# q and k turned by VectorE in blocks of 32x32 instead of by TensorE, in a fused attention and FFN layer

## The chip, the cores and the metric

One core of one Trainium2 chip. The time is the device time of one execution in microseconds (us). Profiles are of one execution each.

## What is computed

x is [2, 1024, 1024] f32. It is normalised along its last axis (xn), and the output is x + attention(xn) + FFN(xn):

```python
qkv = clip(einsum('bsd,ed->bse', xn, Wqkv), -8, 8); q, k, v = split(qkv)
q = layer_norm(q) * q_ln_w + q_ln_b          # over all 1024 columns; k alike
q, k, v -> [B, S, 32 heads, 32]
scores = einsum('bqhd,bkhd->bhqk', q, k) * 32**-0.5 + slope[h] * (key - query), causal
out = einsum('bhqk,bkhd->bqhd', softmax(scores), v)
attention = einsum('bsd,ed->bse', out, Wout)
FFN = einsum('bsi,oi->bso', xn, mean|W| * sign(W)) + bias
```

## The kernel before

All engines have programs written out by hand, ordered by semaphores. There are 16 token tiles of 128. To keep f32 accuracy, operands are split into a high and a low f16 half, and a product is made of three passes (high-high, high-low, low-high). `product` (line 1029) makes one tile's product: 8 k-tiles x 3 passes x 2 halves of 512 columns, 48 matmuls.

Stages, in order: FFN product (with the input's turn, line 1018); q, then k, then v; attention; output product. The weights of the next stage are split during the present one by ScalarE (`split_hi`, line 648) and VectorE (`split_lo`, line 803); SP loads them (line 382).

**q and k stage**, per token tile: TensorE makes the product of tile t into one of two pairs of PSUM banks, then turns tile t-1's normalised values with 8 f32 transposes of 128x128 (`turn_qk`, line 1076). VectorE clips the product into SBUF (`clipped`, line 890), takes statistics (line 810, then 815), splits a weight piece (803), and normalises in two passes, `xc - mean` times weight (line 911) and times rstd plus bias (line 914). GpSimd makes rstd between (lines 542 and 568). Of the turned tile in PSUM ScalarE makes the high f16 half (`turn_out`, line 698) and stores it from its own DMA queue (700); VectorE makes the low half (`turned_low`, line 900), which SP stores (`store_low`, line 421). The turned layout in DRAM is `[head, 64 rows, token]`, the 64 rows being 32 dimensions, each high and low: pieces of 128 tokens, 256 bytes.

**Stacks.** Attention works on 16 groups (batch, 4 heads). For each, a stack `ks` (rows: k high, k high or low, k low, 3 rows of the position term) and `qs` (q high and low, q high again, ones, and one row of negated maxima) is loaded from DRAM by `load_part` (line 357), 8 DMAs a group in runs of 1024 tokens for k and 512 for q. Three stacks exist. At the start of the V stage SP issues, in order, the last low half of k, waits for it, six fills of constant rows (483, 484), waits, 24 loads for three stacks, and then the first store of v (`store_v`, line 440), for which the third tile's clip in the V stage waits. In attention ScalarE issues group n+2's loads, one part after each chunk of group n from chunk 3 on.

**Attention**, per group n: 12 chunks of keys against query halves. TensorE makes transposed scores (`scores`, line 1160, and a mask matmul, 1163), ScalarE exponentiates (740), TensorE multiplies by v (1183, 1188, 1193), with GpSimd adding some chunks (599). Between, TensorE makes the natural scores of group n+1 (`maxima`, line 1099), and VectorE reduces them to row maxima (931, 935). The maxima of a query half, 16 rows of 128, are turned (1107, 948) and written by SP as one row of the `qs` stack, `row_a_in` (445) and `row_b_in` (449); group n+1 can't start without its row a, and its fifth chunk (chunk 4) needs row b. SP also carries the softmax sums: `sums_out` (455), a reciprocal on VectorE (978), a store to DRAM (460) and a broadcast load (463). VectorE's program has the reciprocals at fixed places among the maxima. GpSimd normalises (578) and makes the low half of the attention output (588). The order in SP's program is:

```python
            for n in range(GROUPS):
                row_b_in(n)
                if n > 0:
                    sums_out(blk_no(n - 1, 1))
                    recips_in(blk_no(n - 1, 1))
                if n < GROUPS - 1:
                    row_a_in(n + 1)
                sums_out(blk_no(n, 0))
                recips_in(blk_no(n, 0))
```

Of the kernel before, what the change touches and what calls it, by code (L numbers as in the profile page):

```python
# [10 lines left out]
P = 128  # L11
# [11 lines left out]
GH = 4  # L23
# [43 lines left out]
def build_program(nc, x, wqkv_t, wout_t, wffn_t, ffn_bias, q_w, q_b, k_w, k_b,  # L67
                  ident_h, ident_b, mask_nat, mask_tr, q_fill, k_fill, k_extra, out):
    q_scr = nc.dram_tensor("q_scr", [HEADS, 2 * DH, TOK], F16, kind="Internal").ap()
    k_scr = nc.dram_tensor("k_scr", [HEADS, 2 * DH, TOK], F16, kind="Internal").ap()  # L70
# [6 lines left out]
    with ctx:  # L77
# [34 lines left out]
        xl = [f16(split_at + s * DM + DM // 2, DM) for s in range(2)]  # L112
        at += 2 * DM
# [18 lines left out]
        qs = [f16(a, GH * SEQ).rearrange("p (a j t) -> p a j t", a=2, j=GH) for a in stack_at]  # L132
        ks = [f16(a + GH * SEQ // 2, GH * SEQ).rearrange("p (j t) -> p j t", j=GH) for a in stack_at]
# [24 lines left out]
        idf = f32(at, P); at += P  # L158
# [42 lines left out]
        idf_set = sem("idf_set")  # L201
# [134 lines left out]
        LOADS = 8  # L336

        def load_part(eng, n, part):

            b, h0, s = n // NG, n % NG * GH, n % STACKS  # L340
            toks = slice(b * SEQ, (b + 1) * SEQ)
            hq = q_scr[h0:h0 + GH, :, toks].rearrange("j r t -> r j t")
            hk = k_scr[h0:h0 + GH, :, toks].rearrange("j r t -> r j t")
            if part < 2:
                dst, src = ks[s][part:2 * DH:2], hk[0:2 * DH:2]
            elif part == 2:
                dst, src = ks[s][2 * DH:3 * DH], hk[1:2 * DH:2]
            elif part == 3:
                dst, src = ks[s][3 * DH:3 * DH + 3], k_extra[h0:h0 + GH].rearrange("j r t -> r j t")
            else:  # L350
                a, again = (part - 4) // 2, part % 2
                cols = slice(a * HALF, (a + 1) * HALF)
                if again:
                    dst, src = qs[s][2 * DH:3 * DH, a], hq[0:2 * DH:2, :, cols]
                else:
                    dst, src = qs[s][0:2 * DH, a], hq[:, :, cols]
            eng.dma_start(dst, src).then_inc(stack_ld[s], 16)  # L357

        def stack_loaded(n):
            return 16 * LOADS * (n // STACKS + 1)  # L360

# [10 lines left out]
        def _(sp):  # L372
# [43 lines left out]
            def rows_of(scr, part, t):  # L416
                return scr.rearrange("(m h) (d s) t -> s (h d) m t", h=GH, s=2)[part][:, :, bass.ds(t * P, P)]

            def store_low(blk, t, p):
                sp.wait_ge(lo_done, ready(t + NT * (blk - 1)))  # L420
                sp.dma_start(rows_of({Q: q_scr, K: k_scr}[blk], 1, t),
                             tl[p].rearrange("p (m t) -> p m t", t=P)).then_inc(tl_st[p], 16)
# [3 lines left out]
            for blk in (K, V):  # L426
                load_w(blk, 0, 0, 0)
                if blk == V:
                    store_low(Q, NT - 1, 1)
                with sp.Fori(0, NT // 2 - 1) as j:  # L430
                    load_w(blk, j * 2 + 1, 1, j)
                    store_low(blk - 1, j * 2, 0)
                    load_w(blk, j * 2 + 2, 0, j + 1)
                    store_low(blk - 1, j * 2 + 1, 1)
                load_w(blk, NT - 1, 1, NT // 2 - 1)
                store_low(blk - 1, NT - 2, 0)
# [6 lines left out]
            def row_a_in(n):  # L443
                sp.wait_ge(nat_out, use(n, ROWA) + 1 + RB)
                sp.dma_start(qs[n % STACKS][P - 1:P, 0], row_a[n % 2][0:16, :]).then_inc(rowa_ld, 16)

            def row_b_in(n):
                sp.wait_ge(nat_out, (use(n + 1, ROWB) if n < GROUPS - 1 else use(GROUPS, 0)) + 1 + RB)
                sp.dma_start(qs[n % STACKS][P - 1:P, 1], row_b[n % 2][0:16, :]).then_inc(rowb_ld, 16)
# [28 lines left out]
            store_low(K, NT - 1, 1)  # L478
# [3 lines left out]
            for s in range(STACKS):  # L482
                sp.dma_start(qs[s][3 * DH:P].rearrange("p a j t -> p (a j t)"), q_fill).then_inc(fill_ld, 16)
                sp.dma_start(ks[s][3 * DH:P].rearrange("p j t -> p (j t)"), k_fill).then_inc(fill_ld, 16)
# [47 lines left out]
        def _(pool):  # L532
            pool.sem_inc(rstd_done, RING)
# [28 lines left out]

            for blk in (Q, K):
                def qk_step(t, p, j, first=False):
                    g, q = t + NT * blk, t + NT * (blk - 1)
                    variance_plus(g, p, eps_qk)
                    pool.wait_ge(u_done, slot_free(q))
                    nc.gpsimd.tensor_tensor(rs[p], var_eps[p], expo, ALU.pow).then_inc(rstd_done, 1)  # L568

                tile_loop(pool, qk_step)  # L570

# [65 lines left out]
        def _(act):  # L637
# [56 lines left out]
            def turn_out(scr, q, t, p, stores):  # L694

                act.wait_ge(qt_done, ready(q))
                act.wait_ge(th_st[p], stored(stores))
                nc.scalar.activation(th[p], banks(4 + 2 * p, 2), ACT.Copy).then_inc(hi_done, 1)
                act.wait_ge(hi_done, ready(q))
                act.dma_start(scr.rearrange("(m h) (d s) t -> s (h d) m t", h=GH, s=2)[0][:, :, bass.ds(t * P, P)],  # L700
                              th[p].rearrange("p (m t) -> p m t", t=P)).then_inc(th_st[p], 16)

            act.wait_ge(idh_ld, 16)
            nc.scalar.activation(idf, idh, ACT.Copy).then_inc(idf_set, 1)
# [3 lines left out]
            for blk in (Q, K):  # L708
# [3 lines left out]
                def qk_step(t, p, j, first=False):  # L712
                    q = t + NT * (blk - 1)
                    split_hi(blk + 1, t, p, j)
                    if not first:
                        before = (j if p else j - 1) + NT // 2 * (blk - 1)
                        turn_out({Q: q_scr, K: k_scr}[blk], q - 1, t - 1, 1 - p, before)
                    elif blk == K:
                        turn_out(q_scr, NT - 1, NT - 1, 1, NT // 2 - 1)
# [5 lines left out]
            for t in range(NT):  # L725
                p, j = t % 2, t // 2
                split_hi(WO, t, p, j)
                if t == 0:
                    turn_out(k_scr, 2 * NT - 1, NT - 1, 1, NT - 1)
# [59 lines left out]
        def _(dve):  # L789
            for s in (w_lo, stats, xl_done, xtl_out, mm_out, u_done, lo_done):  # L790
# [105 lines left out]
            def turned_low(q, p, stores):  # L896

                dve.wait_ge(hi_done, ready(q))
                dve.wait_ge(tl_st[p], stored(stores))
                nc.vector.tensor_tensor(tl[p], banks(4 + 2 * p, 2), th[p], ALU.subtract).then_inc(lo_done, 1)  # L900

            for blk in (Q, K):
                def qk_step(t, p, j, first=False):
# [12 lines left out]
                    if not first:  # L916
                        turned_low(q - 1, 1 - p, (j if p else j - 1) + NT // 2 * (blk - 1))
                    elif blk == K:
                        turned_low(q - 1, 1, NT // 2 - 1)
# [3 lines left out]
            def maxima(s, pos):  # L923
# [3 lines left out]
                for i, key, width, col in parts:  # L927
                    at = j * 4 + (i if i < 4 else 16 + i - 4 if key == 0 else 32 + i - 4)
# [15 lines left out]
            def row_out(n, at, row, loads):  # L944

                dve.wait_ge(nat_done, at + 1)
                need(dve, loads, 16 * (n - 1))
# [14 lines left out]
            for t in range(NT):  # L962
# [7 lines left out]
                if t == 0:  # L970
                    turned_low(2 * NT - 1, 1, NT - 1)
# [33 lines left out]
        def _(pe):  # L1005
            for s in (xt_done, qt_done):
                pe.sem_inc(s, RING)
# [32 lines left out]
            def block_product(blk, t, p, between=None):  # L1040
                pe.wait_ge(mm_out, slot_free(t + NT * blk))
                product([ps[:, 2 * p + c, :] for c in range(2)],
                        lambda k, a: xnt[:, bass.ds(t, 1), k, a, :].rearrange("p o c -> p (o c)"),
# [36 lines left out]
            pe.wait_ge(idf_set, 1)  # L1080
            for blk in (Q, K):
                pe.wait_ge(w_lo, ready(NT * blk - 1))

                def step(t, p, j, first=False):
                    block_product(blk, t, p)
                    if blk == K or not first:
                        turn_qk(t + (NT * (blk - 1) - 1), 1 - p)
# [3 lines left out]
            def maxima(s, pos):  # L1091
# [38 lines left out]
            for t in range(NT):  # L1130
                if t == 0:
                    block_product(V, t, 0)
                    turn_qk(2 * NT - 1, 1)
                    continue
# [3 lines left out]
                if t == V_FIRST:  # L1138
                    pe.wait_ge(fill_ld, 16 * 2 * STACKS)
                    pe.wait_ge(lo_done, ready(NT * 2 - 1))  # L1140
# [8 lines left out]
            def scores(n, c, j):  # L1149
# [49 lines left out]
            for n in range(GROUPS):  # L1199
                pe.wait_ge(rowa_ld, 16 * (n + 1))  # L1200
                for c in range(NC):
                    if c == QB_END[0] + 1:
                        pe.wait_ge(rowb_ld, 16 * (n + 1))
# [34 lines left out]
def _constants():  # L1238
# [18 lines left out]

    def bf(v):
# [31 lines left out]
```

## Time and profile before

| | us |
|---|---|
| median of three runs (lowest, highest) | 1409.92 (1408.61, 1413.5) |
| the profiled execution, its own time | 1414.06 |
| its span, first to last instruction | 1412.3 |
| TensorE busy | 1341.1 (95%) |
| VectorE busy | 791.2 (56%) |
| ScalarE busy | 512.0 (36%) |
| GpSimd busy | 446.0 (32%) |

The mean granted TensorE clock was 0.993 of full speed. Engines are PE (TensorE; PEld is its weight load), DVE (VectorE), ACT (ScalarE), POOL (GpSimd) and SP (SyncE, which only issues DMAs); a q behind a name, as in SPq, marks what the queue of that engine issues. Busy shares are averages over stages; what a change in a stage is worth is read from that stage.

### The profile page before, as it was taken

The numbers are of one execution on the slowest core, as the hardware profiler recorded it, in microseconds if no ns is written. First come the engines' busy times: TensorE is split into PE (matmuls) and PEld (weight loads), VectorE is DVE, ScalarE is ACT, GpSimd is POOL, SyncE is SP. The second block draws the span as 40 slices with busy tenths as digits, with TensorE's granted clock in tenths as the row PEclk, the third lists the DMA queues.
The fourth block names the chain that finished last, engine by engine and source line by source line (L and its number), as shares of the span: only waits on it lengthen the run. The fifth ranks groups of instructions, "written<-read, shape, count | busy, mean of one in ns | idle before, by whom it ended". The sixth has DMA issues, their size and how long they took to land.

```text
span 1412.3 us, 36370 instructions
## 1 busy us (share of the span) xinstructions
PE 1341.1 (95%) x15012; PEld 678.3 (48%) x15012; DVE 791.2 (56%) x1794; ACT 512.0 (36%) x1019; POOL 446.0 (32%) x313
## 2 busy tenths in 40 slices
PE   5799999999999999699999999989999999999998
PEld 2344444444454444244345555555555555444443
DVE  4677266655566661112578778878877788201111
ACT  5444111111111110000037767767777777700000
POOL 1222000000000000000005555555544445697665
PEclk9999999999999999899999999999999999999999
DMA  5445122223222225712122333332333332144543
GB/s 214 156 158 198 70 53 67 67 72 77 61 74 67 70 71 134 195 68 81 54 62 57 90 87 81 89 79 79 84 89 87 87 87 60 46 170 136 165 148 119
DMA packets 143799, 137.99 MB, mean 98 GB/s; under 512 B 81969, under 2 KB 110769, under 8 KB 143474
## 3 DMA queue, kind: packets, MB, share of 16 engines
q1 hardware_dynamic: 79199, 99.55, 23.3%
q10 hardware_dynamic: 64467, 36.50, 10.1%
q8 instruction: 104, 1.70, 0.5%
q14 instruction: 29, 0.24, 0.1%
HBM read 93.42 MB, written 42.21 MB: 96 GB/s over the span
## 4 chain that ended last, share of the span: by engine, by line
PE 77%; DMA 9%; DVE 6%; issue 3%; ACT 2%; SPq 2%; POOL 0%; DVEq 0%; ACTq 0%; POOLq 0%
PE ps L1029 49%; PE ps L1099 7%; PE ps L1160 6%; DMA arena<-arena 5%; PE ps L1183 5%; PE ps L1188 4%; DVE ps L931 2%; PE ps L1076 2%; PE ps L1163 1%; DMA arena<-q_scr 1%; SPq L357 1%; PE ps L1193 1%; DMA v_scr<-arena 1%; ACT arena L663 1%; PE ps L1018 1%
## 5 line engine op out<-in xcount | busy, mean ns | idle before, releaser
L1029 PE MATMUL ps<-arena 128*128 128x512 f16 x3584 | 792.7, 381 | 17.9 <-DVE arena L890 11.8
L1029 PEld LDWEIGHTS ps<-arena 128*128 128x128 f16 (+1 forms) x3584 | 348.8, 98 | 437.2 <-issue 17.3
L740 ACT ACTIVATE arena<-ps 128x512 f32<-128x512 f32 (+3 forms) x768 | 339.6, 498 | 146.0 <-PE ps L1163 92.9
L599 POOL TENSOR_TENSOR arena<-arena 128x2048 f32<-128x2048 f32 (+1 forms) x48 | 201.8, 4204 | 390.8 <-ACT arena L740 388.4
L931 DVE CUSTOM_DVE_ANT_0 ps<-ps,arena 128x128 f32<-128x128 f32 (+3 forms) x512 | 239.4, 518 | 58.2 <-PE ps L1099 56.0
L1160 PE MATMUL ps<-arena 128*32 128x512 f16 (+3 forms) x3072 | 255.3, 327 | 4.0 <-ACT arena L740 2.5
L1099 PE MATMUL ps<-arena 127*32 127x512 f16 (+3 forms) x3072 | 237.3, 327 | 14.7 <-DVE arena L931 10.2
L648 ACT ACTIVATE arena<-arena 128x512 f32 (+1 forms) x64 | 40.1, 629 | 492.2 <-DMA arena<-in_wqkv_t 317.0
L890 DVE TENSOR_SCALAR arena<-ps 128x1024 f32<-128x1024 f32 x48 | 58.8, 1225 | 216.9 <-PE ps L1029 187.6
L935 DVE TENSOR_REDUCE arena<-ps 128x1 f16<-128x512 f32 x256 | 162.9, 682 | 15.7 <-PE ps L1099 15.7
L1183 PE MATMUL ps<-arena 128*32 128x512 f32 (+3 forms) x1536 | 160.8, 485 | 0.5 <-issue 0.3
L542 POOL TENSOR_TENSOR small<-small 128x1 f32<-128x1 f32 x48 | 10.0, 207 | 463.1 <-DVE small L815 463.1
L1160 PEld LDWEIGHTS ps<-arena 128*32 128x32 f16 x3072 | 95.8, 96 | 77.0 <-issue 29.1
L1163 PE MATMUL ps<-arena 128*32 128x128 bf16 x2048 | 123.2, 218 | 0.0
L1099 PEld LDWEIGHTS ps<-arena 127*32 127x32 f16 x3072 | 86.8, 96 | 68.0 <-DVE arena L931 21.1
L995 DVE SCALAR_TENSOR_TENSOR arena<-ps,arena 128x1024 f32<-128x1024 f32 x16 | 19.6, 1224 | 154.5 <-PE ps L1029 131.8
L1188 PE MATMUL ps<-arena 128*32 128x512 f32 (+3 forms) x1024 | 96.4, 445 | 0.0
L1163 PEld LDWEIGHTS ps<-arena 128*32 128x32 bf16 x2048 | 63.0, 97 | 51.2 <-issue 32.0
L931 DVE DVE_READ_ACCUMULATOR2_ANT arena<- 128x1 f16 x512 | 73.3, 143 | 0.0
L810 DVE BATCH_NORM_STATS2 small<-arena 128x6 f32<-128x512 f32 x96 | 61.6, 683 | 7.0 <-DMA arena<-in_x 5.9
L911 DVE SCALAR_TENSOR_TENSOR arena<-arena,small 128x1024 f32<-128x1024 f32 x32 | 41.1, 1285 | 33.3 <-POOL small L568 33.3
L803 DVE SCALAR_TENSOR_TENSOR arena<-arena 128x512 f32 (+1 forms) x64 | 44.0, 689 | 15.7 <-DVE small L810 11.6
(53 smaller groups left out, 785.9 us busy)
## 6 DMA issues: line engine op xcount, KB each, us to landing
arena<-in_x SPq DMA_DIRECT2D x32, 512.0 KB, 5.3
arena<-in_wqkv_t SPq DMA_DIRECT2D x48, 256.0 KB, 2.9
arena<-k_scr ACTq DMA_DIRECT2D x39, 256.0 KB
base_scr<-arena SPq DMA_DIRECT2D x16, 512.0 KB, 2.9
v_scr<-arena SPq DMA_DIRECT2D x16, 512.0 KB, 2.9
arena<-r_scr SPq DMA_DIRECT2D x32, 256.0 KB
arena<-base_scr SPq DMA_DIRECT2D x16, 512.0 KB, 4.4
out_dram<-arena SPq DMA_DIRECT2D x16, 512.0 KB, 6.2
```

What stands on the lines that cost most here:

```text
L599: nc.gpsimd.tensor_tensor(acc[:, :, at:HALF], former, p32[k % PSLOTS][:, :, 0:w], ALU.add)\
L740: nc.scalar.activation(p32[k % PSLOTS][:, j, 0:w], ps[:, TRB[x % RB], 0:w], ACT.Exp, scale=SCALE).then_inc(exp_done, 1)
L810: ins = nc.vector.bn_stats(bst[p][:, 6 * c:6 * c + 6], xc[p][:, c * HALF:(c + 1) * HALF])
L890: nc.vector.tensor_scalar(dst[p], banks(2 * p, 2), lim, -lim, ALU.min, ALU.max)\
L931: ins = nc.vector.tensor_tensor_reduce(tile, tile, mnat[:, HALF - width:HALF], scale=-1.0, scalar=3e38, op0=ALU.add, op1=ALU.min, accum_ou ...
L935: ins = nc.vector.tensor_reduce(negm[s % 2][:, at:at + 1], tile, AX, ALU.max, negate=True)
L1029: ins = nc.tensor.matmul(dst[c], lhs(k, a), wparts[:, k, b, c * HALF:(c + 1) * HALF], start=(k == 0 and (a, b) == order[0]), stop=(k == KT ...
L1099: ins = nc.tensor.matmul(ps[r:r + DH, NATB[use(s, pos) % RB], col:col + width], q[0:P - 1, i // 4, j, at:at + DH], k[0:P - 1, j, key:key + ...
L1160: ins = nc.tensor.matmul(dst, k[:, j, t * P + r:t * P + r + DH], q[:, qb, j, at:at + w], start=True, stop=not diagonal)
L1163: ins = nc.tensor.matmul(dst[:, 0:P], idb[:, r:r + DH], mtr, start=False, stop=True)
L1183: ins = nc.tensor.matmul(dst(O_BANK, j, at), v[:, t, j, :], p[:, j, 0:w], start=first, stop=last)
L1188: ins = nc.tensor.matmul(dst(S_BANK, j, at), ones_w, p[:, j, 0:w], start=first, stop=last and qb == 0)
```

## The change

VectorE turns q and k instead of TensorE. Its transpose works on blocks of 32x32 within the tile: partition 32a+d, column 32h+x of the result `ut` holds token 32a+x, dimension d of head h. ScalarE then makes the high half from `ut` in SBUF, GpSimd (no longer VectorE) the low half. The scratch in DRAM becomes `[batch, a, tile, high/low, d, 1024]`, so a store writes rows of 2 KB; a stack's columns run (a, tile, head, 32 tokens), and its load reads pieces of 4 heads x 32 tokens, 256 bytes, in 5 DMAs and not 8. In q and k the product takes the tiles of the two batches in turn (`tile=p * QT + j`). TensorE reads tokens in order from the stack by a three-step pattern (tile, a, token in the block). Rows a and b go into the stack as four DMAs each. The position rows are laid out to suit on the host. The core of the diff:

```diff
-    q_scr = nc.dram_tensor("q_scr", [HEADS, 2 * DH, TOK], F16, kind="Internal").ap()
+    q_scr = nc.dram_tensor("q_scr", [BATCH, P // DH, QT, 2, DH, HEADS * DH], F16, kind="Internal").ap()
...
-        qs = [f16(a, GH * SEQ).rearrange("p (a j t) -> p a j t", a=2, j=GH) for a in stack_at]
+        qs = [f16(a, GH * SEQ).rearrange("p (a t j x) -> p a t j x", a=P // DH, j=GH, x=DH) for a in stack_at]
...
-        LOADS = 8
+        LOADS = 5
+        ROW_PARTS = 16 * (P // DH)
...
+            b, g, s = n // NG, n % NG, n % STACKS
+            cols = slice(g * GH * DH, (g + 1) * GH * DH)
+            both = [scr[b, :, :, :, :, cols].rearrange("a t s d x -> (s d) (a t) x") for scr in (q_scr, k_scr)]
+            q, k = [stack[s].rearrange("p a t j x -> p (a t) (j x)") for stack in (qs, ks)]
+            if part == 0:
+                dst, src = k[0:DH], both[1][0:DH]
+            elif part == 1:
+                dst, src = k[DH:3 * DH], both[1]
             elif part == 2:
+                dst, src = ks[s][3 * DH:3 * DH + 3].rearrange("p a t j x -> p (a t j x)"), k_extra[g]
             elif part == 3:
+                dst, src = q[0:2 * DH], both[0]
             else:
+                dst, src = q[2 * DH:3 * DH], both[0][0:DH]
...
             def row_a_in(n):
                 sp.wait_ge(nat_out, use(n, ROWA) + 1 + RB)
-                sp.dma_start(qs[n % STACKS][P - 1:P, 0], row_a[n % 2][0:16, :]).then_inc(rowa_ld, 16)
+                for a in range(P // DH):
+                    sp.dma_start(qs[n % STACKS][P - 1:P, a, 0:QT // 2].rearrange("p t j x -> p (t j) x"),
+                                 row_a[n % 2][0:16, a * DH:(a + 1) * DH]).then_inc(rowa_ld, 16)
...
+            def low_part(q, p, stores):
+
+                pool.wait_ge(hi_done, ready(q))
+                pool.wait_ge(tl_st[p], stored(stores))
+                nc.gpsimd.tensor_tensor(tl[p], ut[p], th[p], ALU.subtract).then_inc(lo_done, 1)
+
             for blk in (Q, K):
                 def qk_step(t, p, j, first=False):
                     g, q = t + NT * blk, t + NT * (blk - 1)
                     variance_plus(g, p, eps_qk)
                     pool.wait_ge(u_done, slot_free(q))
                     nc.gpsimd.tensor_tensor(rs[p], var_eps[p], expo, ALU.pow).then_inc(rstd_done, 1)
+                    if not first:
+                        low_part(q - 1, 1 - p, (j if p else j - 1) + NT // 2 * (blk - 1))
...
-                nc.scalar.activation(th[p], banks(4 + 2 * p, 2), ACT.Copy).then_inc(hi_done, 1)
+                nc.scalar.activation(th[p], ut[p], ACT.Copy).then_inc(hi_done, 1)
...
-            def turned_low(q, p, stores):
-
-                dve.wait_ge(hi_done, ready(q))
-                dve.wait_ge(tl_st[p], stored(stores))
-                nc.vector.tensor_tensor(tl[p], banks(4 + 2 * p, 2), th[p], ALU.subtract).then_inc(lo_done, 1)
...
+                    dve.wait_ge(u_done, ready(q))
+                    dve.wait_ge(lo_done, slot_free(q))
+                    nc.vector.transpose(ut[p], u[p]).then_inc(qt_done, 1)
...
+            def by_tile(dst):
+
+                return dst.rearrange("p (t a x) -> p t a x", a=P // DH, x=DH)
+
+            def tiles_of(stack, j, at, width):
+
+                return stack[:, :, at // P:(at + width) // P, j].rearrange("p a t x -> p t a x")
...
-            def turn_qk(q, p):
-
-                pe.wait_ge(u_done, ready(q))
-                pe.wait_ge(lo_done, slot_free(q))
-                for m in range(KT):
-                    ins = nc.tensor.transpose(ps[:, 4 + 2 * p + m // 4, (m % 4) * P:(m % 4 + 1) * P],
-                                              u[p][:, m * P:(m + 1) * P], idf)
-                ins.then_inc(qt_done, 1)
...
                     for r in range(0, P, DH):
-                        at = i % 4 * P + r
-                        ins = nc.tensor.matmul(ps[r:r + DH, NATB[use(s, pos) % RB], col:col + width],
-                                               q[0:P - 1, i // 4, j, at:at + DH], k[0:P - 1, j, key:key + width],
-                                               start=True, stop=True)
+                        dst = ps[r:r + DH, NATB[use(s, pos) % RB], col:col + width]
+                        ins = nc.tensor.matmul(by_tile(dst), q[0:P - 1, r // DH, i, j],
+                                               tiles_of(k[0:P - 1], j, key, width), start=True, stop=True)
...
-                    ins = nc.tensor.matmul(dst, k[:, j, t * P + r:t * P + r + DH], q[:, qb, j, at:at + w],
+                    ins = nc.tensor.matmul(by_tile(dst), k[:, r // DH, t, j], tiles_of(q, j, q0, w),
```

## Rows read from the trace of the kernel before

**Rows 1.** The page, part 4: the last chain's shares by line.
```profile
PE ps L1029 49%; PE ps L1099 7%; PE ps L1160 6%; DMA arena<-arena 5%; PE ps L1183 5%; PE ps L1188 4%; DVE ps L931 2%; PE ps L1076 2%; PE ps L1163 1%; DMA arena<-q_scr 1%; SPq L357 1%; PE ps L1193 1%; DMA v_scr<-arena 1%; ACT arena L663 1%; 
```

**Rows 2.** The last chain in order of time: start, us, what.
```profile
184.72 10.36 PE ps L1029 x48
...
330.75 10.37 PE ps L1029 x48
...
344.47 10.53 PE ps L1029 x48
...
513.15 10.37 PE ps L1029 x48
...
570.17 11.35 DMA v_scr<-arena
...
582.82 85.85 PE ps L1029 x390
```

**Rows 3.** Waits of PE, 740 to 1150 us: us in total, times, longest.
```profile
PE ps L1099 <- DVE arena L931: 10.2, 9, 1.8
PE ps L1099 <- DMA arena<-q_scr: 3.0, 3, 1.8
```

**Rows 4.** Timeline of a q tile: start, us, engine, line, operation [idle before].
```profile
318.48 1.04 PE L1076 MATMUL ps<-arena 128*128 128x128 f32 x8
318.68 1.23 DVE L890 TENSOR_SCALAR arena<-ps 128x1024 f32<-128x1024 f32 x1 [2.86 <-PE ps L1029]
...
322.73 0.55 POOL L568 TENSOR_TENSOR small<-small 128x1 f32<-128x1 f32 x1 [0.16 <-POOL small L542]
323.40 1.28 DVE L911 SCALAR_TENSOR_TENSOR arena<-arena,small 128x1024 f32<-128x1024 f32 x1 [1.10 <-POOL small L568]
324.72 1.28 DVE L914 SCALAR_TENSOR_TENSOR arena<-arena,small 128x1024 f32<-128x1024 f32 x1
325.92 1.22 DVE L900 TENSOR_TENSOR arena<-ps,arena 128x1024 f16<-128x1024 f32 x1
```

**Rows 5.** Timeline of attention, and line 941's durations (ns, min/median/max).
```profile
786.40 1.16 POOL L588 TENSOR_TENSOR arena<-arena 128x512 f16<-128x512 f32 x1
786.79 0.79 DVE L941 TENSOR_TENSOR arena<-arena 128x16 f16<-128x16 f16 x1
...
L941 DVE TENSOR_TENSOR arena<-arena x16: 166/210/982, 722.6 to 1210.5; 128x16 f16<-128x16 f16 x16
```

**Rows 6.** Timeline between k and v; v's store from the page, landing last.
```profile
535.82 0.63 ACT L648 ACTIVATE arena<-arena 128x512 f16<-128x512 f32 x1 [9.77 <-DMA arena<-in_wout_t]
...
542.31 0.40 SPq L421 DMA_DIRECT2D k_scr<-arena  x1
...
554.55 2.01 SPq L357 DMA_DIRECT2D arena<-k_scr  x3
...
v_scr<-arena SPq DMA_DIRECT2D x16, 512.0 KB, 2.9
```

**Rows 7.** ScalarE's DMA queue: packets, MB, share; 200:335 (256 B stores), 760.5:766 (512 B loads).
```profile
q10 hardware_dynamic: 12985, 3.27, 10.7%
...
q10 hardware_dynamic: 1088, 0.62, 44.0%
```

**Rows 8.** Timeline of one group: SP's issues and VectorE's reciprocal.
```profile
838.43 0.55 SPq L463 DMA_DIRECT2D arena<-r_scr  x1
839.02 0.55 SPq L445 DMA_DIRECT2D arena<-arena  x1
839.66 0.55 SPq L455 DMA_DIRECT2D arena<-arena  x1
...
846.04 0.25 DVE L978 RECIPROCAL arena<-arena 128x16 f32<-128x16 f32 x1 [2.89 <-DMA arena<-arena]
```

**Rows 9.** The same two in the last group, with no stack loads about.
```profile
1217.65 0.55 SPq L455 DMA_DIRECT2D arena<-arena  x1
...
1219.51 0.25 DVE L978 RECIPROCAL arena<-arena 128x16 f32<-128x16 f32 x1 [8.00 <-DMA arena<-arena]
```

More of the change, by code:

```diff
@@ L112, in build_program @@
         xl = [f16(split_at + s * DM + DM // 2, DM) for s in range(2)]
+        ut = [f32(split_at + s * DM, DM) for s in range(2)]
         at += 2 * DM
@@ L131, in build_program @@
         stack_at = [turn_at - 4 * DM, turn_at, ln_at]
-        qs = [f16(a, GH * SEQ).rearrange("p (a j t) -> p a j t", a=2, j=GH) for a in stack_at]
-        ks = [f16(a + GH * SEQ // 2, GH * SEQ).rearrange("p (j t) -> p j t", j=GH) for a in stack_at]
+        qs = [f16(a, GH * SEQ).rearrange("p (a t j x) -> p a t j x", a=P // DH, j=GH, x=DH) for a in stack_at]
+        ks = [f16(a + GH * SEQ // 2, GH * SEQ).rearrange("p (a t j x) -> p a t j x", a=P // DH, j=GH, x=DH)
+              for a in stack_at]
         PSLOTS = 4
@@ L157, in build_program @@
         ones_w = f32(at, DH); at += DH
-        idf = f32(at, P); at += P
         assert at <= WORDS, at
@@ L532, in _ @@
         def _(pool):
-            pool.sem_inc(rstd_done, RING)
+            for s in (rstd_done, lo_done):
+                pool.sem_inc(s, RING)
             for col, value in ((expo, -0.5), (eps_x, LN_EPS), (eps_qk, LN_EPS * (SX * SW) ** 2),
@@ L715, in qk_step @@
                     if not first:
-                        before = (j if p else j - 1) + NT // 2 * (blk - 1)
-                        turn_out({Q: q_scr, K: k_scr}[blk], q - 1, t - 1, 1 - p, before)
+                        turn_out(blk, q - 1, 1 - p, j if p else j - 1)
                     elif blk == K:
-                        turn_out(q_scr, NT - 1, NT - 1, 1, NT // 2 - 1)
+                        turn_out(Q, NT - 1, 1, NT // 2 - 1)
                 tile_loop(act, qk_step)
@@ L789, in _ @@
         def _(dve):
-            for s in (w_lo, stats, xl_done, xtl_out, mm_out, u_done, lo_done):
+            for s in (w_lo, stats, xl_done, xtl_out, mm_out, u_done, qt_done):
                 dve.sem_inc(s, RING)
@@ L927, in maxima @@
                 for i, key, width, col in parts:
-                    at = j * 4 + (i if i < 4 else 16 + i - 4 if key == 0 else 32 + i - 4)
+                    at = i * GH + j + (GH * QT // 2 if key > 0 and i >= QT // 2 else 0)
                     tile = ps[:, NATB[use(s, pos) % RB], col:col + width]
@@ L946, in row_out @@
                 dve.wait_ge(nat_done, at + 1)
-                need(dve, loads, 16 * (n - 1))
+                need(dve, loads, ROW_PARTS * (n - 1))
                 nc.vector.tensor_copy(row[n % 2][0:16, :], bank16(NATB[at % RB])[0:16, 0:P]).then_inc(nat_out, 1)
@@ L1005, in _ @@
         def _(pe):
-            for s in (xt_done, qt_done):
-                pe.sem_inc(s, RING)
+            pe.sem_inc(xt_done, RING)
             pe.wait_ge(idh_ld, 16)
@@ L1084, in step @@
                 def step(t, p, j, first=False):
-                    block_product(blk, t, p)
-                    if blk == K or not first:
-                        turn_qk(t + (NT * (blk - 1) - 1), 1 - p)
+                    block_product(blk, t, p, tile=p * QT + j)
                 tile_loop(pe, step)
@@ L1130, in _ @@
             for t in range(NT):
[L1131 to L1134, printed above, removed]
                 if t < V_FIRST:
@@ L1256, in _constants @@
         rest = rest - k_extra[:, r].astype(np.float64)
+    k_extra = k_extra.reshape(NG, GH, 3, QT, P // DH, DH).transpose(0, 2, 4, 3, 1, 5).reshape(NG, 3, GH * SEQ)
+    k_extra = np.ascontiguousarray(k_extra)
     def bf(v):
```

75 lines of the change are left out of this document (27 added, 48 removed).

## The prediction

> **What bounds the kernel now.** I read the page first. The chain that ended last runs mostly through TensorE, and the products of line 1029 are half of the span; the f32 transposes of line 1076, which the change takes off TensorE, are 2% of it [rows 1]. Then I read the chain in order of time. In the q and k stages it is nothing but products of 10.36 us: the third of q starts at 184.72 and the sixteenth at 330.75, thirteen steps of 11.23 us. So 0.87 us of each step is the turn on TensorE, and nothing else lies between products. K is alike from 344.47 to 513.15. The V stage has one hole: the fifth V product starts at 582.82, behind a store of v that lands 11.35 us after its issue at 570.17 [rows 2]. In attention I read the waits: TensorE is idle for 10.2 us in twelve groups behind VectorE's line 931, and three times, 3.0 us in all, for a stack's last load of q [rows 3].
>
> **The turn leaves TensorE.** There are 32 turns. Fourteen lie between products of q and fifteen between products of k; two, in the last steps of q and k, lie under the wait for VectorE's split of the next weights (the hole ahead of 344.47), and one lies in the V stage ahead of the hole named above. Those three are worth nothing. If TensorE stays the bound, 29 x 0.87 = 25.3 us go.
>
> **VectorE's loop.** I count from the start C of the clip of line 890 (318.68). The rstd of line 568 ends at C+4.60, line 911 starts at C+4.72, and the old subtraction of line 900 starts at C+7.24 and takes 1.22, so VectorE is free at C+8.46 [rows 4]. It loses line 900 and gets a transpose of 128x1024 f32, which waits for line 914 of its own engine (+0.11, as line 914's start behind 911 is 1.32 for a duration of 1.28, where starts without such a wait overlap by 0.08). No row shows the transpose. By the nearest one, a pass over 1024 f32 elements, it takes 1.22; at half that rate, 2.44; how much quicker it could be doesn't matter, since a product of 10.36 is the floor. I take 1.22: C+8.6, under 10.36.
>
> **GpSimd's new subtraction.** It is queued right behind line 568, and what it waits for (ScalarE's high half of the tile before) has long been done, so it starts at about C+4.65, in the same instant as line 911. Its size: line 588 does the same thing, f16 from f32 and f16, on half as many elements in 1.16, so 2.3 us. Nothing of before shows a long GpSimd operation beside line 911, but one pair of rows shows what to expect: line 941 of VectorE reads two operands from SBUF, takes 0.17 at best, took 0.79 when it started inside line 588, and both ended together (787.56 and 787.58) [rows 5]. So a VectorE operation with two SBUF operands stands still until GpSimd is done, its end 0.15 us ahead of what adding would give. Lines 911 and 914 are such operations. If GpSimd goes first, line 911 in effect starts at C+6.80 and not C+4.72; if VectorE goes first, line 914 is held instead, to the same sum. The transpose then starts at 6.80 + 2.52 + 0.11 = C+9.43 and ends at C+10.65, and the next clip starts at C+10.57: I take a step of 10.6, 0.24 above TensorE's. Fifteen steps of each stage pay that: 7.2 us of the 25.3. The term is -18.1 us, between -25.3 (no blocking) and, with a transpose of 2.44 (step 11.8), +18.
>
> The Trainium skill (SBUF — State Buffer, "SBUF: two separate sides") calls this an exclusive lock on a shared port pair, held for the whole instruction, and names VectorE operations with two SBUF inputs; by that rule the trace agrees (0.79 beside 0.17). A reader of the page alone would add the full 2.3 us, where the sum above adds 2.1.
>
> **From K to V.** Let T be the end of the last k product, 523.52. Before, its last low half is issued at 542.31 (T+18.8), because the turn waits for a whole V product; then fills, first load at 554.55 (T+31.0), and the fifth V product at T+59.3 [rows 2, 6]. After: transpose done at T+10.7; ScalarE's high half 1.1 more and, as its queue has a weight piece ahead that comes about then (535.82, T+12.3, and 1.7 sooner now), T+12; GpSimd 2.3; issue at T+14.4, 4.4 sooner. First load at T+26.6. Now the loads: three stacks are 3 x 6144 pieces of 256 B, where they were 3 x 1152 of 1 and 2 KB. Stores in pieces of 256 B took 0.107 x 16 x 135 us / 12985 = 17.8 ns each; loads in pieces of 512 B took 0.44 x 16 x 5.5 / 1088 = 35.6 ns each [rows 7]. These are my two bounds: 20.5 us to 41.0 us for the three stacks on 16 engines. I take 24 ns, nearer the row with the same length, 27.6 us. The store of v is queued behind them (2.9 [rows 6]), and the clip waits for it (1.3, as 1.23 in [rows 4]): fifth V product at T+58.4, against T+59.3. The term is -1 us, between -8 and +12.5. SP's and ScalarE's fewer load instructions (5 for 8) aren't on the path.
>
> The Trainium skill (DMA: Bandwidth & Descriptors, "Specifications") asks for at least 512 B a transfer for line rate. It speaks against this change, which makes the stores long and the larger number of loads short. The 256 B stores here ran at 256 / 17.8 = 14.4 GB/s an engine, exactly the rate of the 512 B loads, so this trace shows no such penalty; no run yet shows it for loads.
>
> **Attention.** Per group SP does in order: reciprocals in (838.43), row a (839.02), sums out (839.66), 0.64 apart; the sums land only at 846.04, where line 978 has held VectorE for 2.89 us, and the maxima of line 931 behind it are what TensorE waits for [rows 3, 8]. Row a is now four DMAs, so the sums are issued 3 x 0.64 = 1.9 us later. But the same DMA takes 1.86 us from issue to line 978 where nothing is ahead of it (1217.65 to 1219.51) [rows 9], so 4.5 us of the 6.4 is queueing behind the reciprocals' broadcast and ScalarE's stack loads. A later issue eats into that queueing, and the loads now stop at chunk 7 instead of 10. Bounds: nothing, and 1.9 x the 14 groups that load stacks = 27 us. I take a quarter, 0.5 a group, +7. Loads that end three chunks sooner take the three waits for q away: -3. Row b's four DMAs come at a group's start and are wanted at its fifth chunk; the products of four chunks hide them, and without that cover it would be up to 1.9 us a group again.
>
> The products of lines 1099 and 1160 read runs of 32 tokens, 64 B, and write PSUM in order. I cost that at nothing, as the rows have no such read; at 10% more on their 13% of the chain [rows 1] it would be 19 us.
>
> **Sum.** -18.1 - 1 + 7 - 3 = -15 us. The profiled execution took 1414.06 (span 1412.3), the median is 1409.92, 0.3% less; the forecast is 1409.92 - 15 = 1395, its own range 1386 to 1405.
>
> **Rivals.**
> - TensorE stays the bound: GpSimd and VectorE don't collide, or the queueing absorbs row a. -25.3 - 3 = -28, 1382; with loads of 17.8 ns 1375. For it: VectorE has 1.9 us of slack before the collision. Against: [rows 5].
> - The row a issues count in full: -18 - 1 + 27 - 3 = +5, 1415, no change to slightly slower. For it: a strictly serial queue. Against: [rows 9].
> - The loads are slow: 35.6 ns, +13.5 on the forecast, 1408.
> - On the other side, the transpose: at 2.44 us VectorE is the bound at 11.8 a step, +18 + 3 = +21, 1431. It decides from 1.7 us on. For it: 32-bit elements through a block reorder, which no row shows; against: all VectorE passes over f32 here run at one rate. The Trainium skill (Vector Engine (DVE) Microarchitecture Reference, "The reshape front-end and per-opcode configuration") says a transpose sustains one element per cycle per lane; no run here shows it yet.
> - The three-step read slows the attention products by 10%: +19, 1414. It decides from about 8%.
>
> **How the numbers follow.** Forecast 0.43, TensorE-bound 0.20, row a in full 0.11, slow loads 0.06, slow transpose 0.10, slow reads 0.10. A difference under 0.3% (4.2 us) can't be told from none. Faster: the first two and the mildest of the slow reads, 0.65; the same: the slow loads, half of the row a case and a little of the slow reads, 0.14; slower, the rest, 0.21. The range, 1376 to 1418, leaves out the slow transpose, the worse half of the slow reads and the very best case.
>
> **What would show it.** Product starts in q and k 10.6 apart, not 10.36 or 11.8; a transpose near 1.2 us; line 911 or 914 at up to 3.4 us instead of 1.28, ending with GpSimd's subtraction; first stack load about 26.6 and the fifth V product about 58 us after the last k product; sums out issued 1.9 us later behind four row a DMAs, with line 978's wait up by about half a microsecond; no TensorE wait for q; mean durations of lines 1099 and 1160 at 0.327 us as before. The prediction falls if the transpose is far from 1.2, if short loads cost more than 36 ns, or if the wait of line 978 grows by the full 1.9.

## The result, and the profile after

The change makes the kernel slower: 1463.65 us, median of four runs (1462.86 to 1467.21), against 1411.71 for the kernel before (four runs). The ratio is 1.0368, with a 95% interval of 1.0328 to 1.0408. The forecast was 1395 us, with a range of 1376 to 1418, so the result lies outside the range and on the other side of the kernel before. The profiled execution took 1462.86 (span 1460.9), 48.6 us more than the span before. The mean granted TensorE clock was 0.975.

From the page of the changed kernel: busy times, its groups for the moved work, and the landing of the weight pieces:

```profile
PE 1322.9 (91%) x14756; PEld 649.4 (44%) x14756; DVE 846.4 (58%) x1794; ACT 510.4 (35%) x1018; POOL 512.4 (35%) x345
...
L916 DVE SCALAR_TENSOR_TENSOR arena<-arena,small 128x1024 f32<-128x1024 f32 x32 | 96.1, 3003 | 33.4 <-POOL small L578 33.4
...
L571 POOL TENSOR_TENSOR arena<-arena 128x1024 f16<-128x1024 f32 x32 | 68.0, 2124 | 9.6 <-ACT arena L713 9.6
...
arena<-in_wqkv_t SPq DMA_DIRECT2D x48, 256.0 KB, 6.2
```

TensorE is less busy than before (1322.9 us against 1341.1), as it should be, and yet the kernel is longer. No engine's busy time explains that: VectorE's rose from 791.2 to 846.4, but it is only 58% of the span. The last row is the surprise: a weight piece of 256 KB takes 6.2 us from issue to landing, where the page of before has 2.9 in the same row. The new transpose, from the groups by line:

```profile
L923 DVE STREAM_TRANSPOSE arena<-arena 128x1024 f32<-128x1024 f32 x32 | 39.9, 1245 | 1.1
```

**Where the time came.** Both traces are cut at the same three events: the end T of the last k product, the start of the fifth V product, the start of the output product. (T is the start of the last k product plus its duration: 512.98 + 10.52 before, 534.57 + 10.53 after.)

| us | T | T to fifth V product | to output product |
|---|---|---|---|
| before | 523.50 | 59.3 | 656.7 |
| forecast, against before | -18.1 | -1 | +4 |
| after | 545.10 | 80.4 | 662.7 |
| measured, against before | +21.6 | +21.1 | +6.0 |

The differences sum to 48.7, the spans differ by 48.6. The q, k and V stages hold the miss; attention is near its forecast.

**One tile of q, after.** The timeline, to set beside [rows 4]:

```profile
322.41 0.63 ACT L663 ACTIVATE arena<-arena 128x512 f32 x1 [11.08 <-DMA arena<-in_wqkv_t]
...
323.40 0.69 DVE L814 SCALAR_TENSOR_TENSOR arena<-arena 128x512 f32 x1 [2.68 <-ACT arena L663]
324.01 0.20 DVE L826 BATCH_NORM_AGGREGATE small<-small 128x2 f32<-128x12 f32 x1
...
324.56 0.55 POOL L578 TENSOR_TENSOR small<-small 128x1 f32<-128x1 f32 x1
325.07 2.13 POOL L571 TENSOR_TENSOR arena<-arena 128x1024 f16<-128x1024 f32 x1
325.23 3.05 DVE L916 SCALAR_TENSOR_TENSOR arena<-arena,small 128x1024 f32<-128x1024 f32 x1 [1.02 <-POOL small L578]
327.37 0.58 SPq L421 DMA_DIRECT2D q_scr<-arena  x1
...
328.64 0.34 SPq L385 DMA_DIRECT2D arena<-in_wqkv_t  x1
...
332.05 4.27 PE L1030 MATMUL ps<-arena 128*128 128x512 f16 x19 [1.95 <-DVE arena L901]
...
335.04 0.63 ACT L663 ACTIVATE arena<-arena 128x512 f32 x1 [11.05 <-DMA arena<-in_wqkv_t]
```

Read it as a circle. ScalarE splits a weight piece (322.41). VectorE, whose program is in order, waits 2.68 us for that to make the low half of the piece (323.40), and only behind it closes the statistics (324.01). GpSimd makes rstd, and behind it the new low half of the tile before (to 327.20). SP stores that (327.37), and behind the store issues the next weight piece (328.64). This lands when ScalarE takes it at 335.04, 6.40 us after its issue. From 322.41 to 335.04 are 12.63 us, and no product is among them. TensorE, which needs 10.5, waits 1.95 for VectorE's clip. With a landing of 2.9, as before, the same circle would take 6.23 + 2.9 = 9.1 us and would be hidden under the product.

The circle is not new. In the kernel before it stands in the same tile, and VectorE, which starts its part at 321.49, finds the high half ready since 320.80:

```profile
320.17 0.63 ACT L648 ACTIVATE arena<-arena 128x512 f32 x1 [9.87 <-DMA arena<-in_wqkv_t]
...
328.17 0.34 SPq L382 DMA_DIRECT2D arena<-in_wqkv_t  x1
...
331.13 0.63 ACT L648 ACTIVATE arena<-arena 128x512 f32 x1 [9.42 <-DMA arena<-in_wqkv_t]
```

One round was 10.96 us there, of which 0.69 were slack, so it needed 10.3 of a step of 11.23. The change made its work shorter (8.00 to 6.23 us up to the issue of the weight piece) and its landing longer (2.96 to 6.40).

The waits from 180 to 560 us (in total, times, longest) say the same, VectorE's first, then TensorE's:

```profile
DVE arena L814 <- ACT arena L663: 69.8, 28, 2.7
```

```profile
PE ps L1030 <- DVE arena L901: 24.1, 15, 2.2
PE ps L1030 <- DVE arena L814: 19.0, 1, 19.0
```

The chain of waits is no help here unless one knows what it hides. Its pieces in order of time alternate between GpSimd's subtraction and a long "issue", in which SP's two issues and the landing of the weight piece have no row of their own:

```profile
312.48 2.13 POOL arena L571
314.61 9.64 issue
...
325.11 2.09 POOL arena L571
327.20 9.67 issue
```

**Why a landing of 6.4.** The DMA share of a stretch (last but one column) is a mean over 16 engines. While the stores of this tile and the weight piece behind them run:

```profile
330.00:331.00 1.00, 0.10 (x1) 0.00 (x0) 1.00 (x2) 0.00 (x0) 0.00 (x0) 1.00 0.64 215
331.00:334.00 3.00, 1.95 (x9) 0.90 (x10) 2.27 (x3) 0.00 (x0) 0.00 (x0) 1.00 0.23 81
```

The first row has a burst over many engines, which is read here as the weight piece (issued at 328.64) on those that are free. After it, 0.23 of 16 is about four engines busy for three microseconds, at 81 GB/s; the piece is there only when they are done. The view that the store writes has the block `a` as its outermost dimension, and that has four values. The Trainium skill (DMA: Bandwidth & Descriptors, "Why a DMA increments its semaphore by 16 and not by 1") says that a DMA is spread over the largest number of engines, up to 16, that divides the outermost dimension (of more than one value) on both sides. By that rule it is four here, and the trace agrees with its 0.23; the experiments below test it.

**From K to V**, timeline after, to set beside [rows 6]:

```profile
574.78 0.63 ACT L663 ACTIVATE arena<-arena 128x512 f16<-128x512 f32 x1 [10.93 <-DMA arena<-in_wout_t]
...
578.59 0.55 SPq L421 DMA_DIRECT2D k_scr<-arena  x1
...
586.11 0.35 SPq L486 DMA_DIRECT2D arena<-in_q_fill  x1
...
595.87 1.11 SPq L355 DMA_DIRECT2D arena<-k_scr  x2
...
618.53 1.63 SPq L439 DMA_DIRECT2D v_scr<-arena  x1
...
624.24 1.23 DVE L901 TENSOR_SCALAR arena<-ps 128x1024 f32<-128x1024 f32 x1 [36.03 <-DMA v_scr<-arena]
```

The store of the last low half is issued at T+33.5 (before T+18.8, forecast T+14.4). The fills wait for it for 7.5 us, which were 2.7 before (542.31 to 545.01). From the first load to the fifth V product at 625.52 are 29.7 us, where 31.8 were forecast: the short loads are not what is slow. The last tile of k is clipped at T+13.1, where before it was at T, because VectorE is by then one tile behind TensorE.

**Attention**, SP and VectorE in one group, to set beside [rows 8]:

```profile
883.31 3.40 SPq L445 DMA_DIRECT2D arena<-arena  x4
886.81 0.59 SPq L458 DMA_DIRECT2D arena<-arena  x1
...
889.66 0.25 DVE L980 RECIPROCAL arena<-arena 128x16 f32<-128x16 f32 x1 [2.32 <-DMA arena<-arena]
```

Row a takes SP 3.40 us of issuing, the sums follow. They now land 2.85 us after their issue, where they took 6.4 in [rows 8]. Over all of attention VectorE waits a little longer for them, 0.43 us a group, where half a microsecond was forecast (722 to 1240 us before, 771 to 1289 after):

```profile
DVE arena L978 <- DMA arena<-arena: 46.8, 15, 9.5
```

```profile
DVE arena L980 <- DMA arena<-arena: 53.3, 15, 9.5
```

### The profile page after: what moved, and what is told of

The parts are those of the page before. It is cut to its first block, busy times and chain, and to the rows that moved or that the text cites. A ratio compares the mean times of both kernels' runs of the same rounds, so it can differ in the third digit from the quotient of the medians.

```text
span 1460.9 us, 35937 instructions
## 1 busy us (share of the span) xinstructions
PE 1322.9 (91%) x14756; PEld 649.4 (44%) x14756; DVE 846.4 (58%) x1794; ACT 510.4 (35%) x1018; POOL 512.4 (35%) x345
## 3 DMA queue, kind: packets, MB, share of 16 engines
q10 hardware_dynamic: 99566, 36.50, 10.6%
## 4 chain that ended last, share of the span: by engine, by line
PE 47%; issue 32%; POOL 7%; DMA 6%; SPq 4%; DVE 4%; ACT 0%; POOLq 0%; ACTq 0%; DVEq 0%
PE ps L1030 20%; PE ps L1096 7%; PE ps L1151 7%; PE ps L1174 6%; PE ps L1179 5%; POOL arena L571 4%; DMA arena<-arena 3%; DVE ps L935 2%; SPq L445 2%; SPq L355 2%; PE ps L1154 1%; PE ps L1184 1%; POOL small L555 1%; POOL small L551 1%; POOL small L546 1%
## 5 line engine op out<-in xcount | busy, mean ns | idle before, releaser
L1096 PE MATMUL ps<-arena 127*32 127x512 f16 (+3 forms) x3072 | 237.6, 328 | 18.3 <-DVE arena L935 16.9
L1151 PEld LDWEIGHTS ps<-arena 128*32 128x32 f16 x3072 | 95.7, 96 | 79.2 <-issue 29.7
L916 DVE SCALAR_TENSOR_TENSOR arena<-arena,small 128x1024 f32<-128x1024 f32 x32 | 96.1, 3003 | 33.4 <-POOL small L578 33.4
L571 POOL TENSOR_TENSOR arena<-arena 128x1024 f16<-128x1024 f32 x32 | 68.0, 2124 | 9.6 <-ACT arena L713 9.6
```

The costliest lines, as they stand in the source:

```text
L571: nc.gpsimd.tensor_tensor(tl[p], ut[p], th[p], ALU.subtract).then_inc(lo_done, 1)
L916: nc.vector.scalar_tensor_tensor(u[p], xc[p], mv[p][:, 0:1], w, ALU.subtract, ALU.mult)\
L1096: ins = nc.tensor.matmul(by_tile(dst), q[0:P - 1, r // DH, i, j], tiles_of(k[0:P - 1], j, key, width), start=True, stop=True)
L1151: ins = nc.tensor.matmul(by_tile(dst), k[:, r // DH, t, j], tiles_of(q, j, q0, w), start=True, stop=not diagonal)
```

## The experiments

Theory 1: the store in rows of 2 KB runs on four DMA engines, the weight piece queued behind it on those engines lands late, and the circle through the queue sets the step. Theory 2: the collision of VectorE and GpSimd, or VectorE's longer loop, sets it. Theory 3: SP's order alone sets it, on however many engines the stores run. For attention, A: the order in which SP issues row a and the sums counts in full; B: the sums wait in the DMA queues anyway, and the order matters little. Ratios are against the kernel before on the same chip; its median was 1411.71, 1409.84 and 1412.99 us in the three sets of runs, so differences of whole times between sets are uncertain by about 3 us.

**a1_store4**: every store of a half as four DMAs of 32 partitions. Each covers one block, so its outermost dimension of more than one value has 32. Bytes, rows of 2 KB and order stay. The low half's store is shown; ScalarE's store of the high half is cut up in the same way.

```diff
-                sp.dma_start(half_of(blk, p, j, 1), tl[p]).then_inc(tl_st[p], 16)
+                for dst, src in halves_of(blk, p, j, 1, tl[p]):
+                    sp.dma_start(dst, src).then_inc(tl_st[p], 16)
```

> The changed kernel with each store of a high or low half of q and k as four DMAs of 32 partitions, and nothing else. Theory 1 (narrow stores): a store whose DRAM side has the four blocks as its outer dimension runs on few of the 16 DMA engines, the weight piece that SP issues behind it lands after 6.2 to 6.4 us and not 2.9, and the loop weight split, rstd, low half, store, weight load closes at 12.6 us a tile. Then the landing goes back to about 3 us, three more issues cost some 1.5 us, the step falls to about 10.7 us, and the time to 1463.6 - 30 x 1.9 = 1407, or 1402 with the last stores ahead of V quicker too. Theory 2 (only the collision of VectorE and GpSimd sets the step): no change, 1460 to 1470. Theory 3 (SP's order alone, whatever the engines): no change or slower by the extra issues.

Measured: 1392.8 us, ratio 0.9886 (0.9862 to 0.9911), 71 us less than the changed kernel. Timeline and DMA share of a tile:

```profile
301.11 3.05 DVE L924 SCALAR_TENSOR_TENSOR arena<-arena,small 128x1024 f32<-128x1024 f32 x1 [1.02 <-POOL small L583]
303.24 1.81 SPq L426 DMA_DIRECT2D q_scr<-arena  x4
...
305.73 0.37 SPq L389 DMA_DIRECT2D arena<-in_wqkv_t  x1
...
308.57 0.63 ACT L670 ACTIVATE arena<-arena 128x512 f32 x1 [8.71 <-DMA arena<-in_wqkv_t]
```

```profile
305.00:306.00 1.00, 1.00 (x7) 0.45 (x5) 0.97 (x2) 0.00 (x0) 0.00 (x0) 1.00 0.52 131
```

Four stores cost SP 1.2 us more of issuing, and the weight piece lands after 2.84 instead of 6.40. The share of 0.52 is over eight engines' worth. The clips are 10.36 apart, TensorE's own pace, and VectorE's line still takes 3.05 beside GpSimd. T is 498.24, 25.3 before that of the kernel before: the whole turn on TensorE is gained. Theory 1 holds; theory 3, which wanted no gain, falls. The time is below the 1402 of theory 1 because the step is 10.36 and not 10.7: neither the collision nor the extra issues cost anything here.

**a5_store2**: the same with two DMAs of 64 partitions (`STORES = 2`); the outermost dimension of each is two.

> The changed kernel with each store of a half as two DMAs of 64 partitions: the suspected cost made larger. Theory 1: if the outer dimension of the DRAM side sets how many engines a DMA uses, each has two instead of four, the two share them, and the store takes twice as long, some 3.3 us more, so the weight piece lands after some 9.6 us and the step grows to about 16: 1463.6 + 30 x 3.3 = 1563. Theories 2 and 3: one more issue of about 0.4 us, at most 1476.

Measured: 1574.99 us, ratio 1.1163 (1.1133 to 1.1192). From the page, and from the windows of a tile:

```profile
arena<-in_wqkv_t SPq DMA_DIRECT2D x48, 256.0 KB, 9.0
```

```profile
322.00:323.00 1.00, 0.00 (x0) 0.00 (x0) 0.96 (x2) 0.00 (x0) 0.00 (x0) 0.74 0.26 94
323.00:324.00 1.00, 0.94 (x3) 0.40 (x4) 1.00 (x2) 0.00 (x0) 0.00 (x0) 0.50 0.13 51
324.00:325.00 1.00, 1.00 (x4) 0.33 (x3) 0.21 (x1) 0.00 (x0) 0.00 (x0) 0.50 0.13 51
```

0.13 of 16 is two engines, and it stands there from 323 to 328: two DMAs a store, and still only two engines, so both ran on the same two. The landing of the weight piece goes 6.2, 9.0, 2.7 us with one, two and four DMAs: it isn't the size or the number of DMAs that counts, but the engines that each one gets. These rows also give a price: 51 GB/s are 25.5 an engine. A tile stores two halves of 256 KB, so four engines are busy with them for 2 x 262,144 / 102 GB/s = 5.1 us, and two for 10.3 (estimates). The step is 16.1 us: SP's stores are issued at 318.30 and 334.39.

**a2_weights_first**: SP issues each weight piece ahead of the low half's store that it stood behind; the stores stay as the change has them.

```diff
                 load_w(blk, 0, 0, 0)
+                load_w(blk, 1, 1, 0)
...
-                    load_w(blk, j * 2 + 1, 1, j)
+                    load_w(blk, j * 2 + 2, 0, j + 1)
                     store_low(blk - 1, j * 2, 0, j)
-                    load_w(blk, j * 2 + 2, 0, j + 1)
+                    load_w(blk, j * 2 + 3, 1, j + 1)
                     store_low(blk - 1, j * 2 + 1, 1, j)
-                load_w(blk, NT - 1, 1, NT // 2 - 1)
```

> The changed kernel with SP issuing each weight piece of the k and v weights as soon as its staging slot is free, one step ahead of the low half's store that stood before it. Theories 1 and 3: the loop through the store is cut, VectorE's own loop with the collision remains, 10.6 us a step, and the time falls by 30 x 2.0 = 60 us to 1404. Theory 2: the collision sets the 12.6 us, so nothing changes, 1464.

Measured: 1401.79 us, ratio 0.9946 (0.9929 to 0.9963). The clips are 10.36 apart here too. Timeline:

```profile
303.42 0.34 SPq L385 DMA_DIRECT2D arena<-in_wqkv_t  x1
...
309.60 0.63 ACT L663 ACTIVATE arena<-arena 128x512 f32 x1 [2.83 <-DMA arena<-in_wqkv_t]
```

The piece still takes 6.2 us, but it is a tile ahead, so nobody behind ScalarE waits for it: the circle is cut at its other joint. What is left of the slow stores shows between K and V: T to the fifth V product is 63.6 us against 55.6 in a1.

**a3_low_vector**: the low half goes back to VectorE, behind the second normalisation; GpSimd makes none, so there is no collision. The stores stay. Of the edit the line itself is shown; it moves from GpSimd's program to VectorE's.

```diff
-                nc.gpsimd.tensor_tensor(tl[p], ut[p], th[p], ALU.subtract).then_inc(lo_done, 1)
+                nc.vector.tensor_tensor(tl[p], ut[p], th[p], ALU.subtract).then_inc(lo_done, 1)
```

> The changed kernel with the low half made by VectorE from SBUF, where the old kernel's subtraction stood (behind line 914, ahead of the transpose), so nothing long runs on GpSimd. Theory 2: the collision is gone, VectorE's loop is 9.8 us, TensorE is the bound at 10.4, time 1463.6 - 30 x 2.2 = 1398. Theories 1 and 3: line 911's 3.05 us becomes 1.28, but the low half is ready later (two passes of 1.28 and one of 1.22 in place of GpSimd's 2.12), the store and the weight load behind it too, and the loop grows from 12.6 to about 14.4: slower, 1463.6 + 30 x 1.8 = 1518.

Measured: 1516.51 us, ratio 1.0768 (1.0738 to 1.0798). Timeline:

```profile
312.40 0.63 ACT L652 ACTIVATE arena<-arena 128x512 f32 x1 [12.89 <-DMA arena<-in_wqkv_t]
...
315.23 1.28 DVE L911 SCALAR_TENSOR_TENSOR arena<-arena,small 128x1024 f32<-128x1024 f32 x1 [1.01 <-POOL small L572]
...
319.14 0.58 SPq L421 DMA_DIRECT2D q_scr<-arena  x1
...
326.65 0.63 ACT L652 ACTIVATE arena<-arena 128x512 f32 x1 [12.67 <-DMA arena<-in_wqkv_t]
```

Line 911 is back at 1.28, and the kernel is 53 us slower than with the collision. The store comes later in VectorE's order, and the circle grows to 14.25 us. Theory 2, which wanted a gain, falls.

**b2_first_low_vector**: a2 and a3 together.

> Weight pieces ahead of the stores as in the run at 1401.8, and the low half on VectorE besides, so that nothing on GpSimd collides with lines 911 and 914. In the run at 1401.8 the step was 10.36 us, TensorE's own, with the collision (3.05 us instead of 1.28) in it, so I expect that taking the collision away gives nothing: 1400 to 1404 (VectorE 9.8 us a step). If the collision still cost what the prediction said, 0.24 us a step, it would be 7 us less, 1395.

Measured: 1401.21 us, ratio 0.9932 (0.9898 to 0.9967), not told apart from a2 alone (0.9929 to 0.9963). With the circle cut, it makes no difference whether GpSimd or VectorE makes the low half: the collision is worth nothing at a step of 10.36.

**a4_sums_first**: the changed kernel, with the sums of the group ahead of the four DMAs of row a in SP's program.

```diff
+                sums_out(blk_no(n, 0))
                 if n < GROUPS - 1:
                     row_a_in(n + 1)
-                sums_out(blk_no(n, 0))
```

> The changed kernel with SP issuing, in each attention group, the sums of the first half ahead of row a's four DMAs. In the changed kernel row a takes 3.4 us of issues ahead of the sums (883.31 to 886.81), which land 2.85 us after their issue. Theory A (serial issues): the sums leave 3.4 us sooner and land as much sooner, VectorE's wait of about 2.7 us a group at the reciprocal goes, and with it most of TensorE's 15 to 17 us behind line 935: 1463.6 - 15 = 1449. Theory B (queueing): they land as late as the broadcast load and the stack loads ahead of them let them, about 7 us after that broadcast's issue as in both traces, and the gain is under 4 us: 1460 or more.

Measured: 1453.54 us, ratio 1.0291 (1.0252 to 1.0329): 10 us less than the changed kernel, nearer A (1449) than B (1460 or more). TensorE's wait behind the maxima from 740 to 1250 us, in the changed kernel and then here:

```profile
PE ps L1096 <- DVE arena L935: 16.9, 14, 1.9
```

```profile
PE ps L1096 <- DVE arena L935: 8.7, 13, 1.4
```

**c1_before_sums_first**: the same edit on the kernel before, where row a is one DMA.

> The kernel before with the sums ahead of row a, which is one DMA there, 0.64 us of issue. Theory A (serial issues): 0.64 us a group sooner, so at most 8 us: 1402. Theory B (queueing): nothing, 1408 to 1411.

Measured: 1409.56 us, ratio 0.9981 (0.9958 to 1.0004), not told apart from none, as B has it. TensorE's wait behind the maxima went from 10.2 [rows 3] to 7.0.

**b5_store4_first_sums**: the three cures together: stores in four, weights first, sums first.

> All three cures in the changed kernel: stores as four DMAs, weight pieces ahead of the stores, sums ahead of row a. q and k are already at TensorE's step with either of the first two, so against 1392.8 (four DMAs alone) only the attention stage changes: 1378 by theory A of the sums (serial issues), 1390 by theory B (queueing).

Measured: 1382.63 us, ratio 0.9785 (0.975 to 0.982). This beats both kernels, the one before by 2.1% and the changed one by 81 us.

All runs, cut at the same events (profiled executions, us):

| | T | T to fifth V | to output | median |
|---|---|---|---|---|
| before | 523.50 | 59.3 | 656.7 | 1411.71 |
| after | 545.10 | 80.4 | 662.7 | 1463.65 |
| a1, stores in 4 | 498.24 | 55.6 | 663.5 | 1392.8 |
| a5, stores in 2 | 640.98 | 95.8 | 666.5 | 1574.99 |
| a2, weights first | 497.33 | 63.6 | 663.2 | 1401.79 |
| a3, low half on VectorE | 593.49 | 84.7 | 659.7 | 1516.51 |
| b2, a2 and a3 | 499.54 | 64.8 | 664.9 | 1401.21 |
| a4, sums first | 544.68 | 80.1 | 653.2 | 1453.54 |
| c1, before, sums first | 521.89 | 59.1 | 655.1 | 1409.56 |
| b5, all three | 499.44 | 57.1 | 652.6 | 1382.63 |

Six of these kernels (after, a1, a5, a2, a3, b2) have the same program for attention, and their third column lies between 659.7 and 666.5. Each is one execution, so a difference of 3 us in that column says nothing by itself.

## Why the prediction was wrong

**The failed step is "VectorE's loop" and the collision behind it, as the place where the step of q and k is decided.** The prediction took the larger of TensorE's product (10.36) and VectorE's own sum (10.6) as the step. It never wrote down the third circle, weight split, statistics, low half, store, weight piece, although its reading of VectorE's program held most of it and the trace of before has it, at 10.3 us a round. And it named the stores' rows of 2 KB without costing their landing, nor that of the weight piece behind them: both stood in its sum at nothing, and it named no work that would hide them. The step became 12.50 us in q (clips from 193.54 to 356.10, 13 steps) and 12.27 in k (374.14 to 558.21, 15 steps), 49.8 us more than 10.6 would give. The whole miss up to the fifth V product is 61.8 us (39.7 up to T, 22.1 behind it); so four fifths of it are this circle. The clip of the last k tile starts at T+13.1, which is why some of it shows in the second column of the table.

**The turn leaves TensorE: right.** 29 x 0.87 = 25.3 us were worked out; with the circle short again, T comes 25.3 us sooner (a1).

**The collision: right in kind, mis-sized.** Line 916 takes 3.05 where 3.36 at most was forecast, ends 1.0 to 1.1 us after GpSimd's operation as a stall would have it, and delays VectorE by 1.77 a tile, not 2.08. That puts VectorE's sum at 10.65 - 0.31 = 10.3, just under the product. So its 7.2 us were in truth nothing: a2 and b2, with and without the collision, can't be told apart. The transpose, taken at 1.22, is 1.245; GpSimd's subtraction, taken at 2.3, is 2.12.

**From K to V: wrong by 22 us.** Behind T, 13.1 us are the circle. The other 9 come from the slow stores at other places: ScalarE's weight piece comes at 574.78, 7.3 us after its issue, and holds up the last high half; the last store lands in 7.5 us, not 2.7. The loads, at 29.7 us against 31.8, were well sized. With stores on all engines the term is -3.7 (a1), where -1 was forecast.

**Attention: right in kind, +6.0 for +4.** The six runs with this attention program spread from +3.0 to +9.8 in that column, so the size is shown only to a few microseconds. Row a's four DMAs cost 3.40 us to issue and not 2.6, and TensorE's wait for the maxima grew from 10.2 us to 16.9 (15.4 to 19.3 in the five others). No wait for q is left, as forecast. The rival "row a in full" (+27) is excluded. Undoing the order gives 9.5 us back after the change and 1.6 before it (third column, a4 and c1), so the four DMAs cost some 8 us in their old place, with the same uncertainty; TensorE's wait for the maxima says it more firmly, 16.9 to 8.7 after the change and 10.2 to 7.0 before it. Why a stage with row a's four DMAs and sums first is even 2 to 4 us shorter than the one before (653.2 and 652.6 against 655.1 and 656.7) was not tried, and is hardly more than the spread; the waits for q of 3.4 us that c1 still has are of that size.

**The rivals.** The slow transpose, the slow reads (lines 1096 and 1151 take 0.328 and 0.327 us, as before) and the slow loads are excluded. "TensorE stays the bound" is what happens once the circle is cut. None of the rivals was about the stores.

## What to carry to other kernels

Whoever changes the layout of a store changes how many DMA engines it gets: look at the outermost dimension on both sides, estimate its landing again, and that of everything queued behind it. Look for circles through a queue (a load is issued behind a store, the store waits for some work, and that work waits for the load before): they stand in no engine's busy time, so add up one round of each and hold it against the step. A prefetch belongs ahead of the store in the queue, and a value that a busy engine waits for ahead of a row that is wanted later.

## What the runs showed of the hardware

- A DMA whose outermost dimension is 4 ran on about four engines (share 0.23), one with 2 on two (0.13), a store cut into four pieces of 32 partitions on more (0.52). In rows of 2 KB an engine moved 25.5 GB/s, where pieces of 256 bytes ran at 14.4 [rows 7].
- A store on four engines delays a load issued behind it although the other twelve are free: 6.40 us to landing, against 2.84 behind a store that is spread. After 331 us only about four engines work (0.23 after 0.64), and the piece is taken once they stop. That it is the load's own share on these four that comes last is argued from this; the rows do not name a packet's DMA.
- VectorE's transpose of 128x1024 f32 in blocks of 32x32 takes 1.245 us; other f32 passes over as many elements take 1.19 to 1.28. Reads in runs of 64 bytes by TensorE cost nothing: a matmul of the attention products takes 0.327 to 0.328 us on average, and took 0.327 before.
- A VectorE pass of 1.28 us with two operands in SBUF, begun 0.16 us after a GpSimd pass of 2.13, took 3.05 and ended 1.08 after it.
- In a5, TensorE stood still from 320.05 to 323.06 us; the granted clock was 0.74 in 322 to 323 and then 0.50, the lower of its two levels (1.2 GHz), for two microseconds. Products in that run took up to 13.4 us, and not 10.5. As a step was 16.1 us, a product still ended in time. In the changed kernel (0.975 granted) some products took 12.22 us, as that at 307.13, and others 10.53 with TensorE idle for 1.95 before them; no product lies in the circle, so the clock isn't what sets its step.
